# The per-pair attention temperature of a gated cross-attention block: where the network's output is clipped

## What is computed

```python
feats = jnp.stack([mean_sim, max_sim, entropy_proxy], axis=-1)
hidden = jax.nn.gelu(_linear(feats, w1, b1), approximate=False)
hidden = jax.nn.gelu(_linear(hidden, w2, b2), approximate=False)
log_t = jnp.clip(_linear(hidden, w3, b3), LOG_T_MIN, LOG_T_MAX)
t = jnp.exp(log_t)[..., None]
attn_scores = qk / (2.0 * t)
attn = jax.nn.softmax(attn_scores, axis=-1)
```

## Time and profile before

| what | value |
|---|---|
| median of 3 runs | 799.12 us (798.35 to 801.06) |
| the profiled execution | 797.28 us, its span 795.5 us |
| PE busy | 705.6 us (89%) |
| DVE busy | 715.6 us (90%) |
| ACT busy | 688.6 us (87%) |
| POOL busy | 521.0 us (65%) |
| distance from one pair's `ct` to the next (starts 318.15 and 356.17) | 38.0 us |
| granted TensorE clock, 100 to 675 us | 1.00 |

### The profile page before, as it was taken

The page is one execution under the profiler, slowest core; times in us unless marked ns, Lnnn a source line. Parts: engine busy times, 40 slices in busy tenths (PEclk is TensorE's granted clock), DMA queues, the critical chain, the costliest instruction groups (busy, mean ns, idle before and its releaser), DMA issues.

```text
span 795.5 us, 20958 instructions
## 1 busy us (share of the span) xinstructions
PE 705.6 (89%) x7127; PEld 475.4 (60%) x7127; DVE 715.6 (90%) x1479; ACT 688.6 (87%) x1482; POOL 521.0 (65%) x983
## 2 busy tenths in 40 slices
PE   6568899999999999999999999999998888777886
PEld 4334466666666676667676667676665556443444
DVE  5779899989999999999999999899999968798996
ACT  1478899899999999999999999999998997678884
POOL 4747666767777767666667676767663254476985
PEclk9666899999999999999999999999999999899999
DMA  9997747464767575766555666746472123157566
GB/s 206 204 264 164 194 127 151 108 131 124 153 122 145 126 144 125 151 121 138 146 128 136 136 123 130 142 121 145 117 136 53 47 73 118 33 139 165 134 164 175
DMA packets 148889, 108.50 MB, mean 136 GB/s; under 512 B 56992, under 2 KB 145184, under 8 KB 148768
## 3 DMA queue, kind: packets, MB, share of 16 engines
q1 hardware_dynamic: 143630, 101.98, 57.3%
q10 hardware_dynamic: 5152, 5.19, 2.8%
HBM read 49.54 MB, written 12.85 MB: 78 GB/s over the span
## 4 chain that ended last, share of the span: by engine, by line
PE 49%; DVE 22%; ACT 20%; issue 7%; DMA 2%; ACTq 1%; POOL 0%; SPq 0%; DVEq 0%; POOLq 0%
PE p_m L1415 10%; PE p_o L1337 9%; PE p_s L1317 7%; ACT ex L1183 7%; PE p_t L1358 6%; ACT pt L1173 5%; PE p_m L1396 4%; DVE kst L1019 4%; DVE hmax L1022 4%; PE p_m L1404 4%; DVE stats L894 3%; ACT L1209 3%; DVE nm L913 2%; ACT L1173 2%; PE p_m L1422 2%
## 5 line engine op out<-in xcount | busy, mean ns | idle before, releaser
L1183 ACT ACTIVATE ex<-p_s,nm 112x375 f32<-112x375 f32 x512 | 275.3, 617 | 12.4 <-DVE nm L913 10.5
L1173 ACT ACTIVATE pt<-p_t,ct 128x336 f32<-128x336 f32 x488 | 245.3, 575 | 25.8 <-PE p_t L1358 23.7
L894 DVE BATCH_NORM_STATS2 stats<-ex 112x6 f32<-112x375 f32 x512 | 252.6, 535 | 1.4 <-ACT ex L1183 1.3
L913 DVE TENSOR_REDUCE nm<-p_s 112x2 f32<-112x750 f32 x256 | 236.3, 923 | 1.0 <-PE p_s L1317 1.0
L1317 PE MATMUL p_s<-kst,qst 96*112 96x375 bf16 x512 | 154.5, 348 | 13.2 <-ACT ex L1183 7.1
L1358 PE MATMUL p_t<-qst,kst 99*128 99x112 bf16 x1464 | 114.8, 213 | 5.2 <-ACT pt L1173 4.4
L1358 PEld LDWEIGHTS p_t<-qst,kst 99*128 99x128 bf16 x1464 | 90.7, 98 | 44.0 <-issue 19.7
L1396 PE MATMUL p_m<-wv_sb,ctxt 128*128 128x256 f32 (+1 forms) x384 | 105.8, 398 | 4.3 <-DVE va L846 2.3
L1337 PE MATMUL p_o<-pt,va 128*32 128x112 f32 (+1 forms) x3072 | 101.9, 266 | 1.0 <-ACT ex L1183 0.5
L1415 PE MATMUL p_m<-ctxt,wk_sb 128*128 128x375 f32 x240 | 94.5, 518 | 1.6 <-DVE qf L862 0.9
L1317 PEld LDWEIGHTS p_s<-kst,qst 96*112 96x112 bf16 x512 | 67.0, 139 | 45.2 <-ACT ex L1183 34.4
(11 more groups left out here) (190 smaller groups left out, 1216.6 us busy)
## 6 DMA issues: line engine op xcount, KB each, us to landing
kst<-kp SPq DMA_DIRECT2D x378, 93.8 KB, 3.5
ctxt<-ctxt_dram SPq DMA_DIRECT2D x32, 375.0 KB, 3.9
qbounce<-qp SPq DMA_DIRECT2D x32, 168.0 KB, 2.4
qst<-qbounce SPq DMA_DIRECT2D x32, 168.0 KB, 3.6
qst<-qbounce SPq DMA_DIRECT2D x32, 112.0 KB, 3.4
xm<-x_dram SPq DMA_DIRECT2D x32, 112.0 KB, 2.3
x_dram<-x SPq DMA_DIRECT2D x32, 112.0 KB, 1.9
xt<-x_dram SPq DMA_DIRECT2D x28, 128.0 KB, 3.1
```

The source lines that it names most:

```text
L894: last = nc.vector.bn_stats(stats[:, nb % RING, 2 * pb + i], ex[0:SQ, 2 * (t % 2) + i, :])
L913: nc.vector.tensor_reduce(nm[:, n % RING, 2 * p:2 * p + 2], p_s[t % 2][0:SQ, :, 0:SK], axis=AX.X, op=ALU.max, negate=True).then_inc(s_max, 1)
L1173: nc.scalar.activation(pt[:, (2 * r + i) % 8], st_home(r, i)[:, 0:KC * SQ].rearrange("k (c q) -> k c q", c=KC), ACT.Exp, scale=ct[:, nr % ...
L1183: nc.scalar.activation(ex[0:SQ, 2 * ((t - 1) % 2) + i, :], p_s[(t - 1) % 2][0:SQ, i, 0:SK], ACT.Exp, bias=nm[:, ne % RING, h:h + 1]).then_ ...
```

## The change

The bias is taken out of the copy and put into the bounds: clip(h + b, lo, hi) = b + clip(h, lo − b, hi − b), and exp(ln2 − b − c) takes the bias back in. So DVE clips `t_h3` straight out of PSUM in slot 0 of the odd row, with two bounds per partition (`t_lo`, `t_hi`), and ACT makes `ct` in slot 1 with the bias `b3c` = ln2 − b3. ACT's `lt` and POOL's clip are gone; PE waits for the clip instead of `lt`. POOL makes the three 128x1 columns once, in slot 13, and no longer fills `ln2`.

```diff
...
@@ gpsimd, slot
-                if p == 1 and pair_of(n - 1):
-
-                    j = (n - 1) // 2
-                    pool.wait_ge(s_lt, j)
-                    if j > 1:
-                        pool.wait_ge(s_c, j - 1)
-                    nc.gpsimd.tensor_scalar(ltc[:, :], lt[:, :], LOG_T_MIN, LOG_T_MAX, ALU.max, ALU.min).then_inc(s_ltx, 1)
...
+                    for dst, s in ((b3c, LN2), (t_lo, LOG_T_MIN), (t_hi, LOG_T_MAX)):
+                        nc.gpsimd.tensor_scalar(dst[:, :], b3[:, :], -1.0, s, ALU.mult, ALU.add).then_inc(s_smallw, 1)
...
@@ vector, slot
+                if p == 0 and pair_of(n - 1):
+
+                    j = (n - 1) // 2
+                    if j == 1:
+                        dve.wait_ge(s_smallw, B3)
+                    else:
+                        dve.wait_ge(s_c, j - 1)
+                    dve.wait_ge(s_h3, j)
+                    nc.vector.tensor_scalar(ltc[:, :], t_h3, t_lo[:, 0:1], t_hi[:, 0:1], ALU.max, ALU.min).then_inc(s_ltc, 1)
                 if 0 <= t - 2 < SLOTS * B:
...
@@ scalar, slot
-                if p == 0 and pair_of(n - 1):
-                    act.wait_ge(s_h3, (n - 1) // 2)
-                    if n > 3:
-                        act.wait_ge(s_ltx, (n - 1) // 2 - 1)
-                    nc.scalar.activation(lt[:, :], t_h3, ACT.Identity, bias=b3[:, 0:1]).then_inc(s_lt, 1)
-                if p == 2 and pair_of(n - 1):
-
-                    if n == 3:
-                        act.wait_ge(s_prp, PRP_LN2)
-                    act.wait_ge(s_ltx, (n - 1) // 2)
+                if p == 1 and pair_of(n - 1):
+                    act.wait_ge(s_ltc, (n - 1) // 2)
                     r0 = (n - 3) % RING
-                    nc.scalar.activation(ct[:, r0:r0 + 2].rearrange("p b h -> p (b h)"), ltc[:, :], ACT.Exp, scale=-1.0, bias=ln2[:, 0:1]).then_inc(s_c, 1)
+                    nc.scalar.activation(ct[:, r0:r0 + 2].rearrange("p b h -> p (b h)"), ltc[:, :], ACT.Exp, scale=-1.0, bias=b3c[:, 0:1]).then_inc(s_c, 1)
...
@@ tensor, slot
                 if p == 1 and pair_of(n - 1):
-                    pe.wait_ge(s_lt, (n - 1) // 2)
+                    pe.wait_ge(s_ltc, (n - 1) // 2)
```

More of the change, by code:

```diff
@@ L88, in gated_block @@
         b1, b2, b3 = sb("b1_sb", [DH, 1]), sb("b2_sb", [DH, 1]), sb("b3_sb", [P, 1])
-        gx, tg, ln2 = sb("gx_sb", [P, 1]), sb("tg_sb", [P, 1]), sb("ln2_sb", [P, 1])
+        gx, tg = sb("gx_sb", [P, 1]), sb("tg_sb", [P, 1])
         ident, identb = sb("ident_sb", [P, P]), sb("identb_sb", [P, P], BF16)
@@ L112, in gated_block @@
         hid1, hid2 = sb("hid1", [DH, 2 * H]), sb("hid2", [DH, 2 * H])
-        lt, ltc = sb("lt", [P, 2 * H]), sb("ltc", [P, 2 * H])
+        ltc = sb("ltc", [P, 2 * H])
+        b3c, t_lo, t_hi = sb("b3c", [P, 1]), sb("t_lo", [P, 1]), sb("t_hi", [P, 1])
         ct = sb("ct", [P, RING, H])
@@ L243, in gated_block @@
         s_feat, s_fx, s_fr = sem("s_feats"), sem("s_feat_chain"), sem("s_feat_recip")
-        s_h1, s_g1, s_h2, s_g2, s_h3, s_lt, s_ltx, s_c = (sem(f"s_mlp_{i}") for i in ("h1", "g1", "h2", "g2", "h3", "logt", "clip", "c"))
+        s_h1, s_g1, s_h2, s_g2, s_h3, s_ltc, s_c = (sem(f"s_mlp_{i}") for i in ("h1", "g1", "h2", "g2", "h3", "logt_clipped", "c"))
         s_st, s_e2, s_pv, s_oc = sem("s_scores_t"), sem("s_exp2"), sem("s_pv"), sem("s_o_copied")
@@ L266, in gated_block @@
         WEIGHTS = 11
-        PRP_ONES, PRP_ROWS, PRP_LN2, PRP_VA = 1, 3, 4, 4 + VRING
-        WQ, IDB, TGBO, W1B = 2, 3, 1, 4
+        PRP_ONES, PRP_ROWS, PRP_VA = 1, 3, 3 + VRING
+        WQ, IDB, TGBO, W1B, B3 = 2, 3, 1, 4, 7
         WRAW_AT, ABS_AT, TOT_AT, VA_AT = (6, 1, 3), ((13, 14), (9, 10), (11, 12)), 15, (20, 25, 26)
@@ L549, in _ @@
             pool.wait_ge(s_prp, PRP_ROWS)
-            nc.gpsimd.memset(ln2[:, :], LN2).then_inc(s_prp, 1)
-            pool.wait_ge(s_prp, PRP_LN2)
             def split_k(b, c):
@@ L697, in slot @@
                             pool.wait_ge(s_raw2, 1)
-                        pool.wait_ge(s_prp, PRP_LN2 + i)
+                        pool.wait_ge(s_prp, PRP_ROWS + i)
                         nc.gpsimd.memset(va[i][:, :, :, DK:VW], 1.0).then_inc(s_prp, 1)
@@ L841, in copy_v @@
                     if ch == 0 and b < VRING:
-                        dve.wait_ge(s_prp, PRP_LN2 + b + 1)
+                        dve.wait_ge(s_prp, PRP_ROWS + b + 1)
                     if ch == 0 and b >= VRING:
```

## The result

| | before | after |
|---|---|---|
| median of 22 runs each, us | 801.08 (797.79 to 803.41) | 803.35 (800.28 to 805.22) |
| ratio | | 1.0032, 95% interval 1.0021 to 1.0044 |
| profiled execution, us (its span) | 797.28 (795.5) | 802.47 (800.7) |

The account below looks back on a forecast made before the run. The prediction saw no engine with general room, the chain passing each pair from ACT to PE. Terms +1.20, +0.18, −0.11 and +0.38 summed to +1.65 us, added to the median 799.12: 800.8 us, "the same", range 797.2 to 803.2.

Parts of the forecast that it names:

- The removed memset: On POOL at the start, once, with three added 128x1 operations: below a microsecond, off the chain, so nothing.
- `lt` removed, −0.11 us a pair: ACT, slot 0: dropping the 302 ns instruction lets `pt` start 0.11 us earlier, at most 0.17.
- `ct` moved, +0.21 a pair: ACT, slot 1: `ct` ahead of the ex costs 0.21 us; ex ends 0.10 later, PE waits, +1.20 over twelve pairs.
- rival B: Nothing moves: PE hides 0.1 us of lateness before L1308, only odd pairs count, +0.45, 799.6 us; chance 0.20.
- a load's wait that grows while the period stays: Sign of B at PE's weight load for L1308: its wait for ex grows from 0.17 us, the pair's period stays.
- The clip, 0.09 us: DVE's new 128x32 clip from PSUM, priced by steps between starts at 0.09 us; the copy's 0.37 as upper end.
- Layer 3's wait: DVE's new wait for the last layer, seen at 352.30 with DVE free at 352.29: nothing, at most 0.1 us.
- Cover of 0.38 us at `x`: DVE at L872: 0.28 us idle for PE plus PE's 0.10 lateness would cover the clip's 0.09.
- `x` still waiting for PE, about 0.2 to 0.3 us: Sign expected in the profile after: DVE's `x` (L872) would still wait for PE, by that much.
- The last pair, +0.38: Clip ahead of L977 on DVE makes `xinv`, then ACT's L1219, late: +0.55 us, less 0.17 for `lt`.
- POOL's clip and PE's new wait: POOL loses 16 x 323 ns off the chain; PE's wait before slot 1's `pv` names the clip: nothing from either.
- rival A: ACT's saving counts whole: all 16 pairs gain 0.17 us, −2.7 us, 796.4 us; chance 0.13.

Follow-up runs that it names:

- e4: The changed kernel with buffers at the old addresses and `ct` back in ACT's slot 2, behind slot 1's ex: 798.87 us, ratio 0.9985.
- e1: The changed kernel with every buffer back at its old address, by a 32-byte gap for `ln2` and the three small tensors in `lt`'s room: ratio 1.0002.
- e5: The changed kernel at the old addresses, with a second clip of 29 unread columns on DVE in each pair: ratio 1.0020.
- f3: The changed kernel with a 32-byte gap in front of `kst` and the small tensors in `lt`'s room; `ctxt`, `kp`, `qp` stay 32 bytes lower: ratio 1.0008.
- e7: The kernel before with `ln2`'s 32 bytes directly in front of `kst`: `ctxt`, `kp`, `qp` 32 bytes lower, `kst` and `qst` in place; ratio 0.9995.

## Why the prediction was wrong

- **The step that failed:** "The removed memset [...] once each, are below a microsecond off the chain; nothing too." The sum had no term for what the removal of `ln2`, the tensor that this memset filled, does to the other buffers. Its 32 bytes held `kst` and `qst` on the boundary. By the two-by-two table this is 1.6 to 1.9 us, the larger part of the 2.3 lost. No row of before leads to it; only a comparison of addresses would have raised the question.
- **`lt` removed, −0.11 us a pair:** right. With `ct` in its old place (e4) the period falls from 38.00 to 37.90.
- **`ct` moved, +0.21 a pair:** the edge was right and the size was not: 0.12 (e4 against e1). "Slot 2 on ACT gets back both, but there PE is the chain" is the sentence at fault. The two scores that PE does next (those of slot 3) wait for the ex that ACT does in slot 2. Before, it ends at 357.37 + 1.06 = 358.43, and the weights of the second score stand idle 0.10 us and start at 358.48. After, it ends at 361.63 + 1.05 = 362.68, the weights start at 362.73, and PE's weight load has not stood idle. From PE's load to the next group of `p_o` it is 2.29 us (360.85 to 363.14) instead of 2.36 (356.42 to 358.78). So 0.07 of the lateness comes back one slot on. Forecast +1.20 us for twelve pairs; measured 0.05 for the steady stage, where the removal of `lt` and the new place of `ct` all but cancel. This is **rival B's** outcome, by another mechanism than B's: B let PE hide the lateness at that load, and its sign, a load's wait that grows while the period stays, did come (0.21).
- **The clip, 0.09 us:** wrong, 0.22 to 0.23. The two reads of 224 and 750 columns gave a line whose fixed part was 0.05; at 32 columns the step is 0.14 us above that line. The estimate of 158 ns from the Trainium skill ("VectorE: DVE Perf Modes", section on the TRN2 errata) was nearer, and too low as well; counted at the first two pairs and the last, as the prediction counts the clip, it would have raised the sum by 0.2 us, not 0.1. The upper bound of 0.37 held.
- **Layer 3's wait, nothing and at most 0.1:** 0.06, within the bound.
- **Cover of 0.38 us at `x`:** right in what it said and thinner than it looked. "`x` still waiting for PE, about 0.2 to 0.3 us" did not come: the wait is gone. The rest is small enough that a second clip costs 0.08 (e5).
- **The last pair, +0.38:** wrong; its mechanism gave nothing. The clip did wait and L980 did start 1.00 us late, more than the 0.81 forecast, but L1219 never waited for that `xinv`. In the earlier trace rows it starts 0.31 us after `xinv`'s end, where the releases elsewhere are seen 0.05 us later; that gap was a hint that something else let it go. The end did become longer, by the idle time at `ot` among others, which the prediction had nowhere.
- **POOL's clip and PE's new wait, nothing:** no experiment took them apart; e1 and f3, which have both, bound them together with all else at 0.6 us.
- **The sum** of the computation's own effects was to be +1.65 us. e1 and f3 measured +0.6 us by means, in other places than the sum had them: nothing in the steady stage, and some at the end of the program. With the addresses it became 2.3. That this is near 1.65 is luck.
- **The range.** 803.35 lies just above its end, 803.2, on the side that was given 0.24. Of the 2.55 us between it and the forecast of 800.8, 1.96 are not the change: the kernel before measured 801.08 beside it, where the forecast had started from 799.12. Also, rival A's 796.4 lay outside the range that was said to take in most of A.

## What to carry to other kernels

A change that adds or drops a tensor moves every buffer allocated behind it: before pricing the instructions, print both kernels' addresses, and look at those that many short transfers write. Then compare the transfers' share and landings in the two traces, since a loss that arises at a transfer-bound start says nothing of the instructions that were edited. When versions differ by a few tenths of a per cent, cross the two causes, as in the two-by-two table, and count many executions of each; one profiled execution of the repaired kernel was as long as the one it repaired. And where an instruction goes from one slot to the next, follow the gain into the next slot too: a wait that nothing shows, because it is just met, can take up what comes back.

## What had not been expected of the hardware

- Copies inside SBUF into rows of 750 bytes at a pitch of 768 take about a third longer a packet (80 to 83 instead of 60 to 62 ns) when the rows begin 32, 64 or 224 bytes past a multiple of 256, and 95 ns at 128. The share of the queue they are in rises by 22 to 26%, and by 39% at 128 (75.3 to 77.3 and 85.9 against 61.6% of the engines). Transfers between other buffers in the same queue land later with them, `ctxt` after 4.7 to 6.3 instead of 3.8 us, while its packets last 80 to 85 ns as before.
- Moving `ctxt`, `kp` and `qp` by 32 bytes costs nothing that shows (e7, 62.6%, ratio 0.9995). Nearly all rows of `kp` began off a multiple of 256 already, so this does not tell what an aligned source would be worth. That was not tried.
- A 128x32 clip from PSUM with two bounds from SBUF occupies DVE for 0.22 us in steps, though it is shown as 0.31 long.
- DVE can stand 0.26 to 0.28 us ahead of a copy for nothing that the profile shows, in all nine kernels with the change's computation and one clip, and not in e5, which has 16 clips more, nor in any of the seven with the computation of before. Why is not shown.
